# Z and its turn as full-height products: right factors and small matrices of a ridge attention kernel in one packed step

## The reference, cut to what matters

```python
G = Kc.T @ Kc + RIDGE_EPS * I            # 64 x 64
W = jnp.linalg.solve(G, Kc.T @ Vc)       # 64 x 64
U = U0                                   # first 8 unit vectors
for _ in range(POWER_K):                 # 2
    U, _ = jnp.linalg.qr(W @ U)
Wr = U @ (U.T @ W)                       # rank 8
S_new = DECAY_ALPHA * S + Wr
out = SCALE * (Qc @ S_new)
...
return x + o @ Wo
```

## Time and profile before

| | |
|---|---|
| median of 3 runs | 949.77 us (946.84 to 951.35) |
| the profiled execution | 944.12 us, span 942.3 us |
| PE busy / DVE / ACT / POOL | 85% / 66% / 53% / 24% of the span |
| PE's share of the chain that ended last | 71%, "issue" 9% |

### The profile page before, as it was taken

One profiled execution on the slowest core, in us unless ns is written; L12 is line 12 of the kernel. 1 busy time (PEld: TensorE's weight loads), 2 busy tenths in 40 slices (PEclk: granted clock), 3 DMA queues, 4 the chain that ended last, 5 costly groups with the idle time before them and its releaser, 6 DMA issues.

```text
span 942.3 us, 36291 instructions
## 1 busy us (share of the span) xinstructions
PE 802.9 (85%) x15690; PEld 544.9 (58%) x15690; DVE 624.7 (66%) x1336; ACT 496.6 (53%) x1100; POOL 226.5 (24%) x297
## 2 busy tenths in 40 slices
PE   4999999999989998766767785679896899589896
PEld 2555555665556566655545564457674667467775
DVE  3666596399998999998093844778874113566664
ACT  2954444564555454534433446357575566366765
POOL 4655000101002000001001002543023113255554
PEclk9999999999999998757877779789998999799998
DMA  8544213653567245556446432253436332122210
GB/s 309 161 152 142 86 40 104 185 164 91 186 180 210 79 129 154 159 152 149 100 114 150 148 122 83 67 149 95 114 123 148 89 91 90 32 85 74 80 46 29
DMA packets 174671, 114.57 MB, mean 122 GB/s; under 512 B 134128, under 2 KB 152944, under 8 KB 173488
## 3 DMA queue, kind: packets, MB, share of 16 engines
q1 hardware_dynamic: 168784, 91.00, 35.0%
q0 software_dynamic: 5728, 21.24, 6.9%
HBM read 61.22 MB, written 50.99 MB: 119 GB/s over the span
## 4 chain that ended last, share of the span: by engine, by line
PE 71%; issue 9%; ACT 6%; DVE 5%; DMA 3%; POOL 3%; SPq 1%; POOLq 0%; DVEq 0%; ACTq 0%
PE psum L1281 23%; PE psum L1467 7%; PE psum L1327 5%; PE psum L1535 5%; PE psum L1525 5%; PE psum L1418 3%; PE psum L1505 3%; PE psum L1370 2%; PE psum L1383 2%; PE psum L1357 2%; PE psum L1498 2%; PE psum L1441 2%; PE psum L1405 2%; PE psum L1491 2%; ACT late L997 1%
## 5 line engine op out<-in xcount | busy, mean ns | idle before, releaser
L1281 PE MATMUL psum<-wkv,xhat 128*128 128x512 f32 x512 | 233.6, 604 | 4.3 <-ACT xhat L827 4.3
L1137 DVE SCALAR_TENSOR_TENSOR outer<-work,rd 128x992 f32<-128x992 f32 (+30 forms) x248 | 187.1, 754 | 8.9 <-DVE rd L1131 0.3
L1143 DVE TENSOR_TENSOR work<-work,outer 128x992 f32<-128x992 f32 (+30 forms) x248 | 176.9, 713 | 8.5
L1281 PEld LDWEIGHTS psum<-wkv,xhat 128*128 128x128 f32 x512 | 93.9, 191 | 110.9 <-issue 106.5
L864 ACT COPY kv<-psum 128x512 f32<-128x512 f32 x128 | 75.1, 586 | 123.4 <-PE psum L1281 123.2
L755 POOL TENSOR_TENSOR hsplit<-late,hsplit 128x512 f16<-128x512 f32 x64 | 77.3, 1211 | 185.0 <-ACT hsplit L1002 184.9
L997 ACT ACTIVATE late<-psum,b1c,alpha 128x128 f32<-128x128 f32 x256 | 96.7, 462 | 41.2 <-PE psum L1525 41.1
L1505 PE MATMUL psum<-state,xhat 128*128 128x256 f32 x128 | 38.8, 430 | 47.4 <-DVE state L1199 35.8
L1535 PE MATMUL psum<-s2t,hsplit 128*128 128x256 f16 x512 | 67.4, 288 | 3.5 <-POOL hsplit L755 2.7
L1525 PEld LDWEIGHTS psum<-y3t,s1t 128*128 128x128 f16 x1024 | 57.4, 98 | 12.9 <-issue 12.6
L1327 PE MATMUL psum<-kv 128*64 128x128 f32 x1024 | 63.0, 276 | 0.0
(11 more groups left out here) (129 smaller groups left out, 1303.2 us busy)
## 6 DMA issues: line engine op xcount, KB each, us to landing
gc_d<-gc SPq DMA_DIRECT2D x32, 384.0 KB, 2.5
schur_mem<-gc_d SPq DMA_DIRECT2D x32, 384.0 KB, 4.1
f_d<-late SPq DMA_DIRECT2D x16, 512.0 KB, 3.7
late<-f_d SPq DMA_DIRECT2D x32, 256.0 KB, 2.7
sv_d<-sv SPq DMA_DIRECT2D x16, 384.0 KB, 2.9
lead_d<-work POOLq DMA_DIRECT2D x4, 1024.0 KB, 4.9
schur_mem<-lead_d SPq DMA_DIRECT2D x32, 128.0 KB, 4.4
r_d<-pt SPq DMA_DIRECT2D x16, 256.0 KB, 2.5
```

Source lines behind the costliest of these rows:

```text
L1137: V.scalar_tensor_tensor(out=tile, in0=a[:, t, t + 1:HALF].unsqueeze(2).broadcast_to([P, m, HALF]), scalar=rd[:, t:t + 1], in1=a[:, t, t + ...
L1143: V.tensor_tensor(rest, rest, tile, ALU.subtract).then_inc(swept, 1)
L1281: ins = mm(dst[:], xnt[:, c, t], wkv[:, n, t, BANK * half:BANK * (half + 1)], start=t == 0, stop=t == KT - 1)
```

## The change

M and Z of a pair of heads come from one product. W (for the two heads, by rows) and the zero-padded columns of Y now lie side by side in one tile `w`, 64 + 32 columns; the turned copies lie in `wt`. A product has Y's 32 columns (K = 128, two heads) as its weights and the 96 columns of `w` moving, and two of them (n = 0, 1) add up in PSUM, as M's did. So Z is 16 products per pair of chunks instead of 48, and one bank instead of two. Its output has, by 32 rows, the factors of a pair in 64 columns, then M in 32. One copy (`zm`) drains it, and M is stored from there. ZT no longer transposes: four products with the identity (64 of 128 output rows each) turn the factors. ACT drains W with two copies of half the size, Z with one instead of three, ZT with two instead of four. The columns of Y in `w` are cleared by POOL, after the fourth QT instead of at the start. The tables of weights for Z, ZT and W are new and the planner is run again, with the same rules, so the order of later steps moves.

```diff
-BANKS = dict(... Y=2, YT=1, Z=2, ZT=1, ...
+BANKS = dict(... Y=2, YT=1, Z=1, ZT=1, ...
-PE_WEIGHT = dict(... Z=1.2, ZT=.45, ...
+PE_WEIGHT = dict(... Z=.75, ZT=.5, ...
-ACT_WEIGHT = dict(... W=1.1, Y=.9, YT=1.0, Z=1.2, ZT=1.0, ...
+ACT_WEIGHT = dict(... W=1.2, Y=.9, YT=1.0, Z=.45, ZT=.55, ...
...
-        ww = sb("ww", [P, 2, 2 * PAIRS, HD])
...
+        wmem = sb("wmem", [P, 2 * PAIRS * (2 * HD + HALF)])
+        w = wmem[:, 0:2 * PAIRS * (HD + HALF)].rearrange("p (c k n) -> p c k n", c=2, n=HD + HALF)
+        wt = wmem[:, 2 * PAIRS * (HD + HALF):].rearrange("p (c k n) -> p c k n", c=2, n=HD)
...
-        y2 = sb("y2", [P, 2 * QUADS * 2 * HALF])
+        zm = sb("zm", [P, 2, HD + HALF])
         zt = sb("zt", [P, 2 * QUADS * 2 * HALF])
-        ms = sb("ms", [P, 2, HALF])
...
+                elif step == "QT" and c == 3:
+                    pool.wait_ge(*is_filled("QT", 3))
+                    nc.gpsimd.memset(w[:, :, :, HD:], 0.0).then_inc(cleared, 1)
...
-                nc.scalar.copy(ww[:, c % 2].rearrange("p k n -> p (k n)"), place("W", c)).then_inc(drain("W", c), 1)
+                src = place("W", c).rearrange("p (n t q e) -> p n t q e", n=2, t=2, q=QUADS)
+                nc.scalar.copy(w[:, c % 2, :, 0:HD].rearrange("p (n q) e -> p n q e", n=2), src[:, :, 0])
+                nc.scalar.copy(wt[:, c % 2].rearrange("p (n q) e -> p n q e", n=2), src[:, :, 1]).then_inc(drain("W", c), 1)
...
-                nc.scalar.copy(ms[:].rearrange("p c n -> p (c n)"), place("Z", e)[:, DM:DM + HD])
-                act.wait_ge(*is_filled("YT", e))
-                thin_rows("Z", e)
+                if e:
+                    act.wait_ge(*is_filled("ZT", e - 1))
+                nc.scalar.copy(zm[:].rearrange("p c n -> p (c n)"), place("Z", e)[:, 0:2 * (HD + HALF)]).then_inc(drain("Z", e), 1)
...
             def products(e):
...
-                            at, y = DM + HALF * c, columns(y2, c, q, n)
-                            ins = mm(dst[rows(q), at:at + HALF], y, y, start=n == 0, stop=n == 1)
+                            at = (HD + HALF) * c
+                            ins = mm(dst[rows(q), at:at + HD + HALF], y2(c, q, n), w[:, c, QUADS * n + q], start=n == 0, stop=n == 1)
+                ins.then_inc(fill("Z", e), 1)
+
+            def product_columns(e):
+                dst = begin("ZT", e)
+                pe.wait_ge(*is_drained("Z", e))
                 for c in range(2):
-                    for n in range(2):
-                        for q in range(QUADS):
-                            for b in range(2):
-                                o, at, u = HALF * q, BANK * b + HD * (2 * c + n), RANK * (2 * n + b)
-                                ins = mm(dst[o:o + RANK, at:at + HD], columns(y2, c, q, n)[side(b), u:u + RANK],
-                                         ww[side(b), c, 8 * n + q], start=True, stop=True)
-                ins.then_inc(fill("Z", e), 1)
+                    for a in range(2):
+                        ins = mm(dst[side(a), P * c:P * (c + 1)], zm[:, c, 0:HD], ident[:], start=True, stop=True)
+                ins.then_inc(fill("ZT", e), 1)
```

More of the change, by code:

```diff
@@ L503, in side, with y2, z_columns @@
             return slice(HD * a, HD * (a + 1))
-        def columns(t, c, q, n):
+        def y2(c, q, n):
+            return w[:, c, QUADS * n + q, HD:]
+        def z_columns(c, q, n):
             at = HALF * (2 * (QUADS * c + q) + n)
-            return t[:, at:at + HALF]
+            return zt[:, at:at + HALF]
         HALF_BATCH = CPB // 2
@@ L931, in basis_rows @@
                 if e:
-                    act.wait_ge(*is_filled("ZT", e - 1))
+                    act.wait_ge(*is_filled("YT", e - 1))
                 else:
                     act.wait_ge(cleared, 5)
-                thin_rows("Y", e)
-            def thin_rows(step, e):
-                src = pieces(place(step, e), BANK)[:, :, 0:4 * HD].rearrange("p b (c n e) -> p c b n e", c=2, n=2)
+                src = pieces(place("Y", e), BANK)[:, :, 0:4 * HD].rearrange("p b (c n e) -> p c b n e", c=2, n=2)
                 for c in range(2):
@@ L941, in thin_rows @@
                     ins = nc.scalar.copy(dst, src[:, c])
-                ins.then_inc(drain(step, e), 1)
+                ins.then_inc(drain("Y", e), 1)
             def basis(e):
@@ L947, in basis @@
                     act.wait_ge(*is_filled("BQ", e - 1))
-                else:
-                    act.wait_ge(cleared, 5)
-                turned_rows("YT", e, y2)
-            def turned_rows(step, e, thin_columns):
-                src = place(step, e).rearrange("p (c n q r) -> p c n q r", c=2, n=2, q=QUADS)[:, :, :, :, 0:RANK]
-                dst = thin_columns[:].rearrange("p (c q n u r) -> p c n q u r", c=2, q=QUADS, n=2, u=QUADS)
+                src = place("YT", e).rearrange("p (c n q r) -> p c n q r", c=2, n=2, q=QUADS)[:, :, :, :, 0:RANK]
                 for a in range(2):
                     for n in range(2):
-                        ins = nc.scalar.copy(dst[side(a), :, n, :, 2 * n + a], src[side(a), :, n])
-                ins.then_inc(drain(step, e), 1)
+                        at = HD + RANK * (2 * n + a)
+                        ins = nc.scalar.copy(w[side(a), :, QUADS * n:QUADS * (n + 1), at:at + RANK], src[side(a), :, n])
+                ins.then_inc(drain("YT", e), 1)
             def products(e):
@@ L970, in product_columns @@
                     act.wait_ge(*is_filled("BO", e - 1))
-                turned_rows("ZT", e, zt)
+                src = place("ZT", e)[:, 0:2 * P].rearrange("p (k n a r) -> p k n a r", n=2, a=2, r=RANK)
+                dst = zt[:].rearrange("p (k g r) -> p k g r", g=2 * QUADS, r=RANK)
+                for a in range(2):
+                    ins = nc.scalar.copy(dst[side(a), :, a::6], src[side(a), :, :, a])
+                ins.then_inc(drain("ZT", e), 1)
             def factors(step, e, n):
@@ L1441, in turn_rows @@
                         ins = nc.tensor.transpose(dst[:, at:at + P], thin[:, c, P * n:P * (n + 1)], ident[:])
-                ins.then_inc(fill(step, e), 1)
+                ins.then_inc(fill("YT", e), 1)
             def products(e):
@@ L1466, in factors @@
                         for q in range(QUADS):
-                            ins = mm(dst[rows(q), DM * c:DM * (c + 1)], columns(thin, c, q, n), weights[:, 2 * q + n],
+                            ins = mm(dst[rows(q), DM * c:DM * (c + 1)], thin_columns(c, q, n), weights[:, 2 * q + n],
                                      start=n == 0, stop=n == 1)
@@ L1481, in output_factors @@
                 pe.wait_ge(*is_drained("ZT", e))
-                factors("BO", e, zt, wo)
+                factors("BO", e, z_columns, wo)
             def apply_inverse(r):
@@ L1578, in _ @@
                 elif step == "YT":
-                    turn_rows("YT", c, "Y")
+                    basis(c)
                 elif step == "Z":
@@ L1582, in _ @@
                 elif step == "ZT":
-                    turn_rows("ZT", c, "Z")
+                    product_columns(c)
                 elif step == "BQ":
```

24 lines of the change are left out of this document (12 added, 12 removed).

## The result

The changed kernel takes **919.50 us** (median of 4 runs, 915.86 to 924.63) against 950.56 before (946.84 to 956.23, 4 runs): ratio 0.967 [0.960, 0.975]. In a second set of runs it took 921.98 (6 runs) against 950.58 (11 runs): 0.970 [0.966, 0.975]. The profiled execution after is 924.63 us. The one before (944.12) was among the quickest of its kernel, so these two differ by 19.5 us only. I therefore took two more profiles of the kernel before (spans 950.1 and 954.3) and one of the changed (920.4).

A forecast was written before the change was run, and what follows sets the result against it. TensorE (PE), busy 802.9 of 942.3 us, was taken as the bound. PE terms 6.4 + 0 + 4.3 - 0.8 = 9.9, carried at 80% as 8, plus 5 for moved steps, gave 13 us: 936.8 us, range 926 to 950.

The forecast's parts named there:

- Z's product: PE's 16 Z steps: the new product gains 0.42 or 0.38 us each, 6.4 us in all.
- ZT: PE's turns of the factors, as ordinary products instead of transposes: 0 us, bounds +1.5 and -4.6 over the kernel.
- Instructions: PE's "issue" holes read as waits for instruction blocks: 960 records fewer in Z and ZT gain 4.3 us.
- case C: Rival: granted clock falls in 640 to 800 us to the first stretch's level, costing some 20 us: 957; chance 0.09.
- Case A: Rival: instruction blocks pace the first stretch, 372 to 560 us, at 4.8 us each: 23 us gained, 927; chance 0.12.
- The copies, the single bank and what is carried: ScalarE: W's split copy -0.8 us, shorter Z and ZT copies 0; single bank acts through order only; 9.9 carried as 8.
- the 80%: Share of PE's 9.9 us carried to the kernel, since DVE paces part of 612 to 700 us: 8 us.
- Moved steps: Steps the newly planned order moves, at three places, +6, -3 and +2: together +5 us.
- (1) The last inversion: Last batch: turn 16's decay now ahead of the small inverses on DVE, filling PE's 8.93 us hole: +6, bounds 0 and 9.
- (2) Batch 1: GpSimd: the last sweep's load now precedes the small load, lengthening PE's 11.4 us wait: -3, bounds 0 and -8.
- (3) Batch 2: AT 11 now ahead of Z 11, so GpSimd issues the small load earlier: +2, bounds -2 and 4.

The follow-up runs named there:

- f2: The kernel before with 64 tiny records added ahead of the first transpose, nothing left out; one execution, 957.96 us.
- e1: The changed kernel with the tables of the kernel before, so the old order of steps, Z on two banks; 925.87 us, ratio 0.977 to before.
- e5: The changed kernel in the old order of steps, each product of 96 columns cut into three of 32; 937.62 us, ratio 0.987 to before.
- e3: The changed kernel in its new order, each product of 96 columns cut into three of 32, 1024 records more; 933.13 us, ratio 0.985 to before.
- h1: The kernel before in its own order, a step's 64 factor-product records made four of 128x256, 960 records fewer; 940.38 us, ratio 0.987 to before.
- e2: The kernel before, old products, in the changed kernel's order; first four runs 923.5 to 939.0 us, second set 943.56 us, ratio 0.989 to before.
- g1: The changed kernel with the load of batch 1's last sweep moved back behind the small inverses' store; 924.36 us, ratio 0.972 to before.
- f1: The changed kernel with one more FP32 product of 128x512 ahead of each YT, 32 records; 931.12 us, ratio 0.978 to before.
- e4: The changed kernel with ZT as two full 128x128 transposes of factors copied twice side by side; 920.27 us, ratio 0.969 to before.

## Why the prediction was right and wrong

**Z's product: right.** At full clock 0.46 us less for a step (1.14 to 0.68), at half 0.49 (1.75 to 1.26), for 0.42 and 0.38 forecast: 16 times some 0.47 is 7.5 us for 6.4. What I wrote to watch for was less good: 12 to 14 us of group time for what came as 18.1. A group's busy time holds the tail of the last record of each step and the share at half clock, and neither was in that figure.

**ZT: right within its bounds.** Forecast 0; the lines of YT and ZT went from 24.4 to 23.1 us by the means.

**Instructions: the step that failed.** The sum had 4.3 us for 8 blocks: holes divided by blocks, 0.91 and 0.29 us each. The mechanism was right as far as the holes go (f2), and so nearly were the holes themselves, 6.3 us less in the span. The price was wrong. Three pairs of runs give it without the rest of the change: e1 to e5 1.0%, changed to e3 1.5%, before to h1 1.3%, so **10 to 14 us** for 960 to 1024 records, 1.2 to 1.8 us a block, each of the three give or take 4 to 7. In h1 the array also did some 5 us more work, by the lines of Z, YT and ZT, so that its price is rather higher; in e3 and e5 some 4 us are the cut product's own lines. Where the blocks then fall is in each of the three too (f2). What the term left out is the granted clock of the first stretch: with 960 records fewer, 65 to 82 of some 200 us pass at half clock against 96 to 113, and the lines that were not touched, L1473 among them, are quicker by 8.4 us. I had the clock as a threat only (case C, that it would fall where it was high) and never asked whether it could rise where it was low.

The holes and the clock hang together more closely than I had seen. Between Y 0 and Z 7 the granted clock falls 157 times in the sixteen profiles of this study, and 156 of these falls stand in a hole of PE of over 1 us or at most 2.5 us behind one, 130 of them an "issue" hole; of the 157 rises 3 do. Only 43% of that time lies so close to a hole, so this is not chance. A hole at a block would then cost its own length and, behind it, time at half clock, for which nothing in the 0.91 us a block stood. How much of the half-clock time a removed block gives back is still not shown. The holes' total hardly differs between h1 and the first profile before (50 and 50), h1's half-clock time (79) is below all three, and f2 came to 85 by a shift of the places alone. The size of each hole was not tested either.

**Case A** gave 927 us, since it let blocks pace the whole stretch at 4.8 us each. The time came out below it, but not by its mechanism: no pair of runs gives more than 1.8 us a block.

**The copies, the single bank and what is carried: too low.** With the record count of before the product part is still worth 1.3% (e5), 12 us, where 6.4 + 0 - 0.8, carried at 80%, made 4.5. The array's lines account for 5.1 us of it (50.4 to 45.3 for L1456, L1446 and L1464 with the cut). The rest was not separated: ACT is busy for 7 us less (496.6 to 489.5), and the clock was higher (0.929 for 0.916 over the span, the mean of the runs of either). The single bank has no part in it, since Z holds two banks in e5 as in e1. What fails here by name is the copies of Z and ZT, put at 0, and the 80%; which of them by how much stays open. The 80% had its reason in DVE's pace of 612 to 700 us. From AT 3 to AT 8, which is that stretch, the changed kernel is indeed hardly quicker (55.2 us in both profiles against 55.6 to 58.3), but from Y 0 to Z 7 it is 13 us quicker and from AT 11 to AT 15 6, by the means. A share below one was the wrong way to write that.

**Moved steps: 5 forecast, some 10 alone; on top of the product not clear.** e2 in its second set gives 1.1%. From e1 to the changed kernel it is 0.7%, some 7 us, but the intervals overlap, and the profiles show none of it: from the first Y to the end 567 us for e1 against 569 and 567. By place, e2's second profile against the means before:

(1) The last inversion: AT 15 to AT 18 takes 32.6 us for 35.3, a gain of 2.7 where 6 was forecast. The next wait is where I had put it, at the half that DVE turns (L1232), with 4.0 us. In the changed kernel the hole of 8.93 became 0.7 + 4.0, 4.2 less, and the stretch is 2.2 and 3.1 us shorter in its two profiles: of the 2.4 that I had added for the clock nothing is seen.

(2) Batch 1: 1.7 us longer (22.1 for 20.4) where 3 was forecast. The wait of PE grew by 3.5 us (11.4 to 14.9), inside the 2 to 4 named. g1 shows that the cause is right, and that undoing it gains nothing: what batch 1 gets back, batch 2 pays.

(3) Batch 2: AT 11 to AT 15 takes 85.7 us for 88.1 by the means, 2.4 gained for 2 forecast. AT 11 to AT 12 alone is longer, because steps have moved into it.

These make 3.4 for 5. The other gain of the new order in e2 lies in the first stretch, 3.5 us with 128 records more in it, and the sum had nothing there: I had looked at three places only, of an order that moves from the first Z on. With the new product that gain is not seen: e1 takes 199 us for the stretch, the changed kernel 203 and 201.

**Together.** By the ratios the 3.0% of the change are 1.3 for the product with the old record count (e5), 1.0 for the records (e5 to e1) and 0.7 for the order (e1 to changed): 12, 10 and 7 us, where the sum had 4.5, 3.4 and 5. The forecast left the range on the low side chiefly by the first two: the price of a block, which held the holes alone, and the granted clock, which was set at nothing as a gain without a reason. The 7 us of the order may be less, by the profiles of e1. That the time came near case A's 927 is luck; the sign is not, since every one of these parts has it.

## What to carry to other kernels

Where PE runs dense small records and its page shows "issue" holes in the middle of runs of one line, price a record removed by a run that removes records and little else, not by the holes divided by their number: here 1000 records were worth 10 to 14 us, about as much as all the rest of the packed product. Shift the stream once by some records as well, to see what the places alone are worth. In such a stretch read the granted clock as something that a change can also give back: at 0.72 the lines that a change does not touch have time to gain too. And an order that is planned again is not the sum of the places that one looks at; run the new order with the old code.

## What the runs showed of the hardware that was not expected

Holes of PE without a named cause stand behind weight loads 5584, 5964, 6091, 6217 of the program and keep these counts when 64 records are put ahead. Their spacing is 126 or 127 weight loads or a multiple of that, and the instruction queue moved 125 packets for 15690 of them.

The granted clock fell behind such holes: 156 of 157 falls in the dense stretch of sixteen profiles stand in a hole of over 1 us or at most 2.5 us behind it.

The granted clock of one stretch was higher with fewer records at more array work (h1: 0.81, against 0.74 to 0.78 in the three profiles before), but also with the same work and the places shifted (f2: 0.80). 23 us of long products added moved it little (f1: 0.942 over the span for 0.937).

Sixty-four products with the identity and 64 columns of weights (L1464, 10.6 us for 128 records) do the turns in no time that can be told from that of transposes: with whole transposes of twice the columns (e4) the ratio is 0.969 for 0.970. The Trainium skill, "TensorEngine Tiling (Array Packing)", restrictions, rules column tiling out for the FP32 transpose mode. No run here tried that mode, but what stands in its place costs nothing that these runs can tell.
